# Row maxima of attention scores in four row groups of the array, with permuted heads and stacks of their own

## The reference, as far as it matters

```python
q = (src @ Wq + bq).reshape(B, T, NHEAD, HEAD_DIM)      # 16 heads of 8
scores = jnp.einsum('bqhd,bkhd->bhqk', q, k) * scale
probs = jax.nn.softmax(scores, axis=-1)
out = jnp.einsum('bhqk,bkhd->bqhd', probs, v).reshape(B, T, d)
```

## Time and profile before

| | |
|---|---|
| median of three runs | 2330.1 us |
| span of the profiled execution | 2333.7 us |
| PE busy, mean granted clock | 2126.1 us (91%), 0.964 |
| PE weight loads | 1618.6 us (69%) |
| DVE busy | 1719.7 us (74%) |
| ACT busy | 1454.2 us (62%) |
| POOL busy | 819.1 us (35%) |
| L739 and L741, maxima matmuls | x512 and x512, 137.0 and 135.2 us |
| L1261, their reduction on DVE | x512, 315.9 us |
| L774, probabilities times V | x2048, 139.2 us, 389 ns each |
| DMA | 88.01 MB, 15.4% of 16 engines |

### The profile page before, as it was taken

The page is one execution under the profiler, slowest core; times in us unless marked ns, Lnnn a source line. Parts: engine busy times, 40 slices in busy tenths (PEclk is TensorE's granted clock), DMA queues, the critical chain, the costliest instruction groups (busy, mean ns, idle before and its releaser), DMA issues. The chain is left out here.

```text
span 2333.7 us, 47546 instructions
## 1 busy us (share of the span) xinstructions
PE 2126.1 (91%) x16832; PEld 1618.6 (69%) x16832; DVE 1719.7 (74%) x4431; ACT 1454.2 (62%) x3113; POOL 819.1 (35%) x1204
## 2 busy tenths in 40 slices
PE   4879889999999999999999999999999999998866
PEld 2556667777777777776777777777777777676544
DVE  6666878787887878787787878788797878755433
ACT  3555657677675766767575766767576676754332
POOL 5212332434343433424333333434333342424131
PEclk9979999999999999999999999999999999998777
DMA  5020112121202112120211212110211212010110
GB/s 152 4 47 10 38 35 47 35 48 29 43 17 45 41 36 50 35 47 8 44 37 37 48 36 48 36 37 15 45 40 36 50 35 45 15 46 21 31 34 5
DMA packets 185820, 88.01 MB, mean 38 GB/s; under 512 B 118297, under 2 KB 179873, under 8 KB 180417
## 3 DMA queue, kind: packets, MB, share of 16 engines
q1 hardware_dynamic: 185584, 84.97, 15.4%
HBM read 51.12 MB, written 33.55 MB: 36 GB/s over the span
## 5 line engine op out<-in xcount | busy, mean ns | idle before, releaser
L1186 DVE SCALAR_TENSOR_TENSOR work<-psA,c_conv_w,work 128x255 f32<-128x255 f32 (+2 forms) x810 | 329.2, 472 | 15.6 <-ACT work L926 14.7
L1261 DVE TENSOR_REDUCE nmax<-psB 128x2 f32<-128x512 f32 x512 | 315.9, 679 | 27.5 <-PE psB L741 27.3
L609 PE MATMUL psA<-xnT_a,c_w_in 128*128 128x256 f32 x1088 | 309.9, 409 | 27.7 <-ACT X L950 15.9
L1213 DVE TENSOR_TENSOR att<-att,QK 128x1024 f32<-128x1024 f32 x192 | 235.4, 1253 | 85.4 <-ACT att L963 85.2
L845 PE MATMUL psB<-c_w,hid 128*128 128x128 f32 x2048 | 280.2, 282 | 7.3 <-ACT pt L1009 5.9
L845 PEld LDWEIGHTS psB<-c_w,hid 128*128 128x128 f32 x2048 | 257.8, 194 | 41.1 <-issue 19.0
L1009 ACT ACTIVATE pt<-psB 128x512 f32<-128x512 f32 x512 | 264.4, 606 | 33.0 <-PE psB L760 33.0
L833 PE MATMUL psB<-x1T,c_w 128*128 128x256 f32 x1024 | 276.6, 398 | 6.2 <-ACT hid L1051 5.4
L963 ACT ACTIVATE att<-psA 128x512 f32<-128x512 f32 x384 | 204.5, 610 | 109.7 <-PE psA L650 83.0
L1032 ACT ACTIVATE hid<-psB,c_b 128x256 f32<-128x256 f32 x496 | 210.8, 484 | 57.8 <-PE psB L833 53.6
L609 PEld LDWEIGHTS psA<-xnT_a,c_w_in 128*128 128x128 f32 x1088 | 194.6, 201 | 72.5 <-ACT X L950 24.1
(11 more groups left out here) (246 smaller groups left out, 4275.1 us busy)
## 6 DMA issues: line engine op xcount, KB each, us to landing
qk_scr<-qparts SPq DMA_DIRECT2D x128, 192.0 KB, 2.5
q_stack<-qk_scr SPq DMA_DIRECT2D x96, 192.0 KB
k_stack<-qk_scr SPq DMA_DIRECT2D x32, 576.0 KB
lvl_scr<-work SPq DMA_DIRECT2D x32, 192.0 KB, 5.2
low<-lvl_scr SPq DMA_DIRECT2D x256, 1.5 KB
c_w_in<-in_in_wT SPq DMA_DIRECT2D x1, 2176.0 KB, 9.3
x<-in_x SPq DMA_DIRECT2D x16, 128.0 KB, 4.4
c_w<-in_W SPq DMA_DIRECT2D x2, 1024.0 KB
```

Source lines behind the costliest of these rows:

```text
L609: e.matmul(t[:, 0:T], w_in[:, first + j * P:first + (j + 1) * P], xnT_a[:, :], start=True, stop=True).then_inc(filled[b], 1)
L1186: m = e.scalar_tensor_tensor(out=cv[:, back:], in0=t[:, 0:T - back], scalar=conv_w[:, c, tap:tap + 1], in1=cv[:, back:], op0=ALU.mult, op1 ...
L1213: e.tensor_tensor(att[:, :, :], att[:, :, :], bc(QK[:, kq, :], 1, HG), ALU.mult).then_inc(att_done, 1)
L1261: e.tensor_reduce(nmax[:, i, 2 * h2:2 * h2 + 2], t[:, :].rearrange("p (h k) -> p h k", k=T), AX.X, ALU.max).then_inc(drained[b], 1)
```

## The change

Maxima are made from the two leading parts of q and of k alone: 2 x 2 x 8 = 32 rows instead of 72. Four heads are then worked on in four row groups of 32 rows of the array. For this q and k get stacks of their own, `q_max` and `k_max`, of 128 partitions (four groups) x 4 slots x 256 tokens, loaded by eight DMAs each from the same `qk_scr`, ahead of the old stacks on SP. The columns of Wq and Wk are permuted, so that each group's four heads lie together in DRAM; PLACE tells `es` where a head lies, and the maxima keep the permuted order. smax goes over two slots and, inside, over four groups: matmul v of group g writes half v of bank g. So the order of issue changes too: all four banks' first halves, then all four second halves. smax step 0 waits for the new stacks, es step 0 for the old ones. V9's rows per head are 9 instead of 32 wide, and its setting to 0 goes. `osb` goes: the two operations add onto `xb`, and the third adds the bias. The hop order is as it was.

```diff
+RG = 4
+HPG = NH // RG
+MAXROWS = 4 * AD
+def head_of(g, slot):
+    return 2 * RG * (slot // 2) + 2 * g + slot % 2
+HEADS = [head_of(g, slot) for g in range(RG) for slot in range(HPG)]
+PLACE = [HEADS.index(h) for h in range(NH)]
...
-        V9 = sb("V9", [P, NT, NH, 32])
+        q_max = sb("q_max", [P, HPG, T], BF16)
+        k_max = sb("k_max", [P, HPG, T], BF16)
+        V9 = sb("V9", [P, NT, NH, AD + 1])
...
+                    if u:
+                        e.wait_ge(*full(attn_hop("smax", 3, u - 1), RG - 1))
+                    e.wait_ge(qk_stored[k], (16, 48)[k] * (u + 1))
+                    for half in range(2):
+                        for g in range(RG):
+                            e.dma_start((q_max, k_max)[k][32 * g + 16 * half:32 * g + 16 * half + 16, :, :].rearrange("p s t -> p (s t)"),
+                                        dram(qk_scrd[k], (3 * AD * NH * T * half if k else 0) + HPG * T * g,
+                                             [[NH * T, 2 * AD], [1, HPG * T]])).then_inc(max_loaded[k], 16)
                     e.wait_ge(pool_setup, 2)
                     if u:
                         e.wait_ge(*full(attn_hop("es", 3, u - 1), 3))
-                    e.wait_ge(qk_stored[k], (16, 48)[k] * (u + 1))
...
                     if k == 0:
-                        e.wait_ge(qk_stacked[0], 48 * (au + 1))
-                        e.wait_ge(qk_stacked[1], 16 * (au + 1))
+                        e.wait_ge(max_loaded[0], 2 * RG * 16 * (au + 1))
+                        e.wait_ge(max_loaded[1], 2 * RG * 16 * (au + 1))
                     i = k // 2
-                    for j in range(4):
-                        h = 2 * (4 * (k % 2) + j)
-                        t, b, u = bank(hop, j)
-                        if u:
-                            e.wait_ge(drained[b], u)
-                        e.matmul(t[:, 0:T], q_stack[0:ROW_MAX, h, i * P:(i + 1) * P], k_stack[0:ROW_MAX, h, :],
-                                 start=True, stop=True)
-                        e.matmul(t[:, T:2 * T], q_stack[0:ROW_MAX, h + 1, i * P:(i + 1) * P], k_stack[0:ROW_MAX, h + 1, :],
-                                 start=True, stop=True).then_inc(filled[b], 1)
+                    for v in range(2):
+                        slot = 2 * (k % 2) + v
+                        for g in range(RG):
+                            t, b, u = bank(hop, g)
+                            if v == 0 and u:
+                                e.wait_ge(drained[b], u)
+                            m = e.matmul(t[:, v * T:(v + 1) * T], q_max[32 * g:32 * g + MAXROWS, slot, i * P:(i + 1) * P],
+                                         k_max[32 * g:32 * g + MAXROWS, slot, :], start=True, stop=True)
+                            if v == 1:
+                                m.then_inc(filled[b], 1)
...
                     if k == 0:
+                        e.wait_ge(qk_stacked[0], 48 * (nth[hop] + 1))
+                        e.wait_ge(qk_stacked[1], 16 * (nth[hop] + 1))
                         e.wait_ge(max_stacked, 16 * (nth[hop] + 1))
...
+                        p0, p1 = PLACE[h], PLACE[h + 1]
-                        e.matmul(t[:, 0:T], k_stack[:, h, kt * P:(kt + 1) * P], q_stack[:, h, :], start=True, stop=True)
+                        e.matmul(t[:, 0:T], k_stack[:, p0, kt * P:(kt + 1) * P], q_stack[:, p0, :], start=True, stop=True)
...
-                            m = e.matmul(t[32 * j:32 * j + 32, 0:T], V9[:, kt, 4 * g + j, :], pt[:, j % 2, :],
+                            m = e.matmul(t[32 * j:32 * j + AD + 1, 0:T], V9[:, kt, 4 * g + j, :], pt[:, j % 2, :],
...
-                    e.scalar_tensor_tensor(out=osb[:, 0, :], in0=t[:, 0:P], scalar=rms[:, 0:1], in1=b_out[:, :],
+                    e.scalar_tensor_tensor(out=xb[:, 0, :], in0=t[:, 0:P], scalar=rms[:, 0:1], in1=xb[:, 0, :],
...
-                    e.tensor_tensor(xb[:, :, :], xb[:, :, :], osb[:, :, :], ALU.add).then_inc(*own.step())
+                    e.tensor_tensor(xb[:, :, :], xb[:, :, :], bc(b_out[:, :], 1, NT), ALU.add).then_inc(*own.step())
...
-                        e.memset(V9[:, :, :, :], 0.0).then_inc(*own.step())
-                        e.wait_ge(*own.now())
...
-        "Wq": f(a[pf + "Wq"].reshape(HID, NH, AD).transpose(0, 2, 1)).reshape(HID, P),
+        "Wq": f(a[pf + "Wq"].reshape(HID, NH, AD)[:, HEADS].transpose(0, 2, 1)).reshape(HID, P),
```

More of the change, by code:

```diff
@@ L357, in build @@
         max_stacked = sem("max_stacked")
+        max_loaded = [sem("q_max_loaded"), sem("k_max_loaded")]
         xn_ready = sem("xn_ready")
@@ L758, in _ @@
                             e.wait_ge(drained[b], u)
-                        e.matmul(t[:, 0:T], k_stack[:, h, kt * P:(kt + 1) * P], q_stack[:, h, :], start=True, stop=True)
-                        e.matmul(t[:, T:2 * T], k_stack[:, h + 1, kt * P:(kt + 1) * P], q_stack[:, h + 1, :],
+                        e.matmul(t[:, 0:T], k_stack[:, p0, kt * P:(kt + 1) * P], q_stack[:, p0, :], start=True, stop=True)
+                        e.matmul(t[:, T:2 * T], k_stack[:, p1, kt * P:(kt + 1) * P], q_stack[:, p1, :],
                                  start=True, stop=True).then_inc(filled[b], 1)
@@ L1231, in _ @@
                     e.wait_ge(filled[b], u + 1)
-                    e.scalar_tensor_tensor(out=osb[:, 0, :], in0=t[:, 0:P], scalar=rms[:, 0:1], in1=b_out[:, :],
+                    e.scalar_tensor_tensor(out=xb[:, 0, :], in0=t[:, 0:P], scalar=rms[:, 0:1], in1=xb[:, 0, :],
                                            op0=ALU.mult, op1=ALU.add).then_inc(*own.step())
-                    e.scalar_tensor_tensor(out=osb[:, 1, :], in0=t[:, P:T], scalar=rms[:, 1:2], in1=b_out[:, :],
+                    e.scalar_tensor_tensor(out=xb[:, 1, :], in0=t[:, P:T], scalar=rms[:, 1:2], in1=xb[:, 1, :],
                                            op0=ALU.mult, op1=ALU.add).then_inc(drained[b], 1)
                     e.wait_ge(*empty(("outp", 0, n, 0)))
-                    e.tensor_tensor(xb[:, :, :], xb[:, :, :], osb[:, :, :], ALU.add).then_inc(*own.step())
+                    e.tensor_tensor(xb[:, :, :], xb[:, :, :], bc(b_out[:, :], 1, NT), ALU.add).then_inc(*own.step())
                 elif what == "fn" and k == 0:
@@ L1520, in lay_out @@
         "gamma": a[pb + "gamma"], "beta": a[pb + "beta"],
[L1521 to L1523 removed]
+        "bq": f(a[pf + "bq"].reshape(NH, AD)[HEADS].T).reshape(P, 1),
+        "bk": f(a[pf + "bk"].reshape(NH, AD)[HEADS].T).reshape(P, 1),
+        "Wq": f(a[pf + "Wq"].reshape(HID, NH, AD)[:, HEADS].transpose(0, 2, 1)).reshape(HID, P),
+        "Wk": f(a[pf + "Wk"].reshape(HID, NH, AD)[:, HEADS].transpose(0, 2, 1)).reshape(HID, P),
         "W1": f(a[pf + "W1"].transpose(1, 0, 2)),
```

7 lines of the change are left out of this document (2 added, 5 removed).

## The result

The changed kernel takes 2375.93 us in the median of 4 runs (2363.96 to 2382.97) against 2329.91 us (4 runs): a ratio of 1.0192, 95% interval 1.0158 to 1.0226. It is slower by 46 us, where 16.6 were forecast, and lies outside the range. The profiled execution took 2382.97 us, with a span of 2381.2.

What follows compares the result with a forecast made beforehand. DVE's reductions were taken to hold PE up at the maxima hops. Layer 0 +15.1, V's table -2.6, DMAs +1.7 and seams +2.4 gave +16.6 us on 2330.1: 2346.7 us, range 2320 to 2368.

Steps and rivals of the forecast that it cites:

- The form: Maxima hops on PE: four row groups take 0.21 us plus 0.25 for edges, 0.46 a hop, a saving of 0.41.
- Layer 0: Layer 0's hops 1 to 3: late first bank delays DVE, 1.29 us a turn, 0.76 with half clock; +15.1 us.
- Layer 1: Layer 1's four maxima hops: PE waits for DVE anyway and the first bank is in time; 0 us gained or lost.
- Rival 4: Ahead of layer 0's stretch at lower clock, PE idles longer; four more half-clock turns, +7 us, 2354 us; 8%.
- DMAs and seams: 16 more DMAs a unit on SP, +1.7 us in the last two units; six seams between hops, +2.4 us.
- V's table: L774's weights shrink from 32 to 9 columns: 20 ns less for the first load of each of 128 hops, -2.6 us.
- Rival 1: Layer 1's four hops: PE's saving counts, 64 hops x 0.41 = -26 us, 2304 us; 12%.
- Rival 3: Maxima hops: row groups take turns or each drains the other, +19 us on the forecast, 2366 us; 10%.
- Rival 2: Behind layer 0's hop 3, DVE's wait for POOL absorbs the first bank's delay: no change, 2332 us; 25%.
- permutation and residual: L1232, L1234 and L1237 keep number and shapes, heads only change addresses, L1237 needs no own buffer: 0 us.

Runs made afterwards that it cites:

- group-major: The changed kernel with its two issue loops swapped, so each bank gets both halves before the next bank: 2337.7 us, ratio 1.0044 to the kernel before.
- half-major in layer 0 alone: The changed kernel, keeping first halves of all four banks, then second halves, only in layer 0; layer 1 finishes each bank in turn: 2359.6 us, 1.0128.
- the version at 1.0014: The changed kernel finishing each bank in turn, its maxima by 72-row matmuls from the old stacks, new loads made but not read: 2331.9 us, 1.0014.

## Why the prediction was wrong

**Direction and mechanism held, the size did not.** Slower, at 61%, and by the order of issue: group-major takes 38 of 46 us away. The forecast was +16.6 us, and the 46 lie outside its range.

**The form: right.** 0.46 us a hop, as measured in sum. The Trainium skill's "TensorEngine Tiling (Array Packing)", Key Properties, says that a change of tiling mode drains the engine. For four row groups this case agrees: the next matmul of the full array starts only 0.06 us after the eight have ended (1010.54 to 1010.60). For column groups, where the prediction saw agreement too, it is less clear: L759 starts 0.07 us before the end that the earlier trace rows gives for L774's matmuls, though later than their spacing would allow.

**Layer 0: right within a quarter.** For a turn without half clock it had 1.29 us; half-major in layer 0 alone adds 1.01 to such a turn, cleaned. DVE's waits ahead of hops 1, 2 and 3 are 0.45, 0.39 and 0.38 us there, where it had 0.53, 0.30 more and 0.46. In turns with half clock the forecast had less, 0.76; they were not measured apart. That the changed kernel's +1.21 against the kernel before lies close to 1.29 is luck: layer 1's share is in it, and V's narrow table takes some off.

**Layer 1: the step that failed.** "The first bank is also in time in each", 0 us lost. I checked that for hop 0 and took it over to the others. In hop 1 the fourth bank is busy while DVE is free, and the trace of the kernel before showed it: ACT's copy ended at 1132.34, DVE had begun at 1132.22. DVE waits 0.25 us, L822 0.35 us more than with the other order, and a turn is 0.37 longer with this alone, cleaned (0.49 as it stands): 5.6 us in 15 turns where the forecast had 0.

**Half clock: the term that was mis-sized.** Rival 4 had four more turns with such a stretch, 4 us at 0.57 each, for +7 us, at 8%, and apart from the forecast, whose sum has nothing for it. Eleven of 13 turns had one, before 6, and mostly twice or three times as long: 61 us more. At about 0.2 us each, from the fit above, that is 12 to 14 us on top of the delay. So rival 4 had too little half clock and charged it at some 0.4 us per us, twice what the fit gives. Windows of one turn (length, busy of PE, PEld, DVE, ACT, POOL, granted clock), first of the changed kernel, from layer 0's third hop on:

```profile
1895.20:1898.60 3.40, 2.38 (x15) 0.97 (x13) 3.01 (x6) 1.46 (x4) 0.00 (x0) 0.97 0.02 5
1898.40:1905.20 6.80, 6.80 (x24) 5.96 (x24) 6.06 (x22) 4.30 (x7) 3.19 (x5) 0.50 0.00 0
```

and the same place in the kernel before:

```profile
1866.20:1869.60 3.40, 3.30 (x20) 2.07 (x19) 3.38 (x7) 2.34 (x6) 0.00 (x0) 1.00 0.00 0
1869.60:1876.40 6.80, 6.47 (x36) 5.12 (x35) 5.96 (x22) 5.46 (x12) 3.20 (x5) 1.00 0.01 4
```

PE was busy 2.38 of 3.4 us where it had been 3.30, and the 1.2 GHz level followed: PE then did 24 matmuls in 6.8 us instead of 36. That PE's work in the hops shifts the half clock was seen three times (81.9 to 54.6, 41.0 to 10.2, and 41.0 to 0 with 72-row matmuls). The order shifts it as well, and the mean granted clock over all executions has the two side by side: in group-major order 0.968 with 72-row matmuls and 0.957 with row groups, in half-major order 0.958 and 0.947. It is not shown how much of the 46 us it is: no run took it away and left the rest.

**The tail and the head.** For DMAs and seams I had 1.7 + 2.4 us; the tail grew by 12.9. The wait from q's store to the first maxima matmul grew by 2.3 and 3.4 us in the two last units (the last: 2253.11 to 2267.21 before, 2291.95 to 2309.40 after). Eight issues take 3.56 us, not 3.0, and k's eight stand in front in full. The waits sum to 5.7 us where I had 1.7. The order has its part too: 276.5 in group-major with the same DMAs. Tails of single executions differ by several us (284.8 with 72-row matmuls), so the split between the two stays open, as does the head's 3.4.

**V's table.** -2.6 us forecast, -7 measured. The load's 20 ns were right, and so was the 0.16 us a turn (0.14, cleaned). The rest of the 7 us is not this term and stays open; the one profiled execution had fewer held turns and less half clock.

**Rival 1** (PE's saving counts) fell clearly: 3.3 us of PE's work a turn less do not shorten a turn without half clock (132.14 us against 132.02). **Rival 3** fell with the 0.46 us. **Rival 2** did not hold: the delays went through.

**What adds up.** In ratios, which are differences of medians and good to some 3 to 9 us each: V's table -7 us (0.9969), DMAs, permutation and residual +10 (1.0014), row groups +7 (1.0044), the order +34 (1.0192). The split between the second and the third is the least certain, since the version at 1.0014 also waits for the old stacks.

## What to carry to other kernels

When several buffers are filled in rounds, the first is complete only after every buffer's wait has been passed; finish each buffer before waiting for the next one, as here the array overlapped just as well. Check every place that such an order touches, not only the first of them, and let a delay count through any stretch in which the next engine has no gap. Before a few tenths of a microsecond are put down to an edit, look whether some instruction of another line has two durations. Time saved on an engine that then only waits is worth nothing, and here even brought a lower clock.

## What the runs showed of the hardware

- Eight bf16 matmuls of 32 rows and 256 columns in four row groups need 0.46 us up to the next matmul of the full array, in either order of issue; 0.88 for eight of 72 rows.
- Four loads of 32 partitions and 64 KB were followed by their first matmul 6.0 us behind the last issue's end; eight of 16 partitions and 32 KB by 1.45 us. Halving the number of DMAs in this way cost the kernel 15 us.
- The outermost size of the source set the cost, not the bytes: from the first issue to the first matmul 5.1 us with 16 rows, 8.4 with 2 x 8 rows (same bytes and count), 8.5 with four loads of 2 x 16. One issue took 0.42 us with 16 rows and 0.59 with either of the others. The first shape left 16 packets of 4 bytes a load, the others 2.
- A shift of 0.33 us at one hop, which began with a wait of 0.25 us on DVE, was still whole 60 us later (0.36).
- A DVE addition of 128x6 elements and a POOL product of 128x256 started within 20 ns of each other. In some turns of a kernel the addition took 0.17 us, in others 0.75, and then it ended 0.02 us behind the product. That was worth about 0.58 us a turn.
- With the same order of issue the mean granted clock fell by 0.011 when four row groups replaced 72-row matmuls, which left PE less to do (0.968 to 0.957 and 0.958 to 0.947).
- A weight load of 9 columns takes 90 ns, of 32 columns 109.
